# Turning chunk 2 by halves, summing one half row-block on VectorE, and another order of the first slots

## The reference

```
rowsum = adj.sum(axis=1)
d = where(rowsum > 0, rowsum ** -0.5, 0)
h = maximum(layernorm(x), 0)                      # eps 1e-5
out = relu((d[:, None] * adj * d[None, :]) @ h @ W + b)
return x + out
```

## Time and profile before

| | |
|---|---|
| median of 3 runs | 393.66 us |
| the profiled execution | 393.01 us, of it the span 391.2 us |
| TensorE (PE) busy | 383.5 us, 98% |
| VectorE (DVE) busy | 317.9 us, 81% |
| ScalarE (ACT) busy | 288.7 us, 74% |
| GpSimd (POOL) busy | 115.0 us, 29% |
| read from and written to HBM | 151.5 MB, 387 GB/s over the span |

### The profile page before, as it was taken

The page is one execution under the profiler, slowest core; times in us unless marked ns, Lnnn a source line. Parts: engine busy times, 40 slices in busy tenths (PEclk is TensorE's granted clock), DMA queues, the critical chain, the costliest instruction groups (busy, mean ns, idle before and its releaser), DMA issues. The chain is left out here.

```text
span 391.2 us, 5139 instructions
## 1 busy us (share of the span) xinstructions
PE 383.5 (98%) x1754; PEld 319.9 (82%) x1754; DVE 317.9 (81%) x312; ACT 288.7 (74%) x286; POOL 115.0 (29%) x253
## 2 busy tenths in 40 slices
PE   8998999999999999999999999999999999999995
PEld 8886888888888888888888888888888888888884
DVE  6839966899686899958689995868899497889996
ACT  2889898788787878679878867978886793346533
POOL 2470335653121226114235811422520144000000
PEclk9999999999999999999999999999999999999999
DMA  7999999999999999999999999999999965997665
GB/s 296 427 421 426 426 424 427 425 429 428 422 423 424 427 427 429 420 426 424 424 428 426 428 419 428 425 425 427 428 426 429 404 229 220 394 372 255 214 169 207
DMA packets 24216, 151.86 MB, mean 388 GB/s; under 512 B 3328, under 2 KB 3328, under 8 KB 7552
## 3 DMA queue, kind: packets, MB, share of 16 engines
q1 hardware_dynamic: 24192, 151.55, 94.5%
HBM read 147.33 MB, written 4.22 MB: 387 GB/s over the span
## 5 line engine op out<-in xcount | busy, mean ns | idle before, releaser
L441 ACT ACTIVATE hi<-at,s 128x1024 fp32r<-128x1024 f32 x112 | 122.9, 1144 | 44.5 <-issue 32.5
L928 PE MATMUL moved<-hi,G 128*128 128x512 f32 x384 | 149.6, 390 | 1.5 <-DVE acc L729 1.5
L930 PE MATMUL moved<-hi,G 128*128 128x512 f32 x384 | 149.4, 389 | 0.0
L929 PE MATMUL moved<-lo,G 128*128 128x512 f32 x384 | 149.4, 389 | 0.0
L713 DVE SCALAR_TENSOR_TENSOR lo<-at,s,hi 128x1024 fp32r<-128x1024 f32 x112 | 140.8, 1278 | 9.1 <-ACT hi L441 9.1
L732 DVE TENSOR_TENSOR acc<-moved,acc 128x1024 f32<-128x1024 f32 x84 | 102.7, 1223 | 50.5 <-PE moved L930 50.5
L431 ACT ACTIVATE nat<-nat 128x2048 f32<-128x2048 f32 x64 | 122.1, 1908 | 7.8 <-DMA nat<-in_adj 7.8
L928 PEld LDWEIGHTS moved<-hi,G 128*128 128x128 f32 x384 | 72.1, 188 | 17.0 <-DVE acc L729 1.9
L930 PEld LDWEIGHTS moved<-hi,G 128*128 128x128 f32 x384 | 72.1, 188 | 15.0
L929 PEld LDWEIGHTS moved<-lo,G 128*128 128x128 f32 x384 | 72.1, 188 | 14.9
L601 POOL TENSOR_TENSOR row_sum<-part 128x1 f32<-128x1 f32 x32 | 17.9, 561 | 183.2 <-ACT nat L431 183.0
(11 more groups left out here) (75 smaller groups left out, 253.3 us busy)
## 6 DMA issues: line engine op xcount, KB each, us to landing
nat<-in_adj SPq DMA_DIRECT2D x64, 1024.0 KB, 13.8
at<-in_adj_t SPq DMA_DIRECT2D x64, 1024.0 KB, 12.4
acc<-in_x SPq DMA_DIRECT2D x4, 512.0 KB, 7.1
nat<-d_dram SPq DMA_DIRECT2D x2, 1024.0 KB, 5.8
nat<-in_x_t SPq DMA_DIRECT2D x4, 512.0 KB, 6.0
turned<-in_x_t SPq DMA_DIRECT2D x4, 512.0 KB, 6.9
out<-nat SPq DMA_DIRECT2D x4, 512.0 KB, 5.1
turned<-in_x SPq DMA_DIRECT2D x3, 512.0 KB, 14.7
```

Source lines behind the costliest of these rows:

```text
L441: nc.scalar.activation(hi[g % RING][:, 2 * c:2 * c + 2, :], at[g % LA][:, 2 * c:2 * c + 2, :], ACT.Copy, scale=s[:, j:j + 1]).then_inc(hi_ ...
L928: nc.tensor.matmul(into[:, f, :], big, hi[g % RING][:, t, :], start=begins, stop=False)
L929: nc.tensor.matmul(into[:, f, :], big, lo[g % RING][:, t, :], start=False, stop=False)
L930: mm = nc.tensor.matmul(into[:, f, :], small, hi[g % RING][:, t, :], start=False, stop=ends)
```

## The change

Chunk 2 joins the chunks that are turned and copied in parts, by halves; TensorE turns its halves between the products of chunk 1, and ScalarE copies them around the rounding of W. Half row-block 3 is summed by VectorE (`sum_early`, with a semaphore of its own, which every waiter for sums adds to its wait). ScalarE's opening is written out anew: chunk 3's G is rounded between the two halves of slot 0, and VectorE's rest of it stands between the first and the second low part. VectorE makes three low parts ahead of the first panel's copy, where it made four, and stays one behind the former order up to slot 2; the rest of chunk 4 moves from the first half of slot 2's turn to the second. GpSimd makes the rstd of chunks 1 to 4 behind the scales of row-blocks 0 and 1.

```diff
+BY_VECTOR = (3,)
-AT_ONCE = {0: 1, 1: 2}
+AT_ONCE = {0: 1, 1: 2, 2: 2}
...
         def wait_summed(eng, m):
-            eng.wait_ge(nat_summed, m + 1)
+            dve_part = len([e for e in BY_VECTOR if e <= m])
+            at_least(eng, nat_summed, m + 1 - dve_part)
+            at_least(eng, dve_summed, dve_part)
...
             def take_part(c, t):
                 last = t + AT_ONCE[c] == BW
+                at_least(act, hW_done, c - 1)
...
-            for t in range(BW):
-                take_part(0, t)
-            take_part(1, 0)
-            take_part(1, 2)
-            round_w()
-            for c in range(AHEAD - 2):
-                if c == 2:
-                    sum_nat(2)
-                round_raw(c)
-                if c < 2:
-                    sum_nat(c)
-                if c + 2 < FIRST_PART:
-                    take_turned(c + 2)
-                else:
-                    take_high(c + 2)
-                if c == 2:
-                    sum_nat(3)
-            round_slot(0)
+            for c in range(OWN):
+                if c == 2:
+                    round_raw(0)
+                for t in range(0, BW, AT_ONCE[c]):
+                    take_part(c, t)
+                    if (c, t) == (2, 0):
+                        round_w()
+            sum_nat(0)
+            round_raw(1)
+            take_turned(3)
+            sum_nat(1)
+            round_raw(2)
+            take_high(4)
+            sum_nat(2)
+            round_tile(0, 0)
+            round_raw(AHEAD - 2)
+            round_tile(0, 1)
             round_slot(1)
-            round_raw(AHEAD - 2)
             round_raw(AHEAD - 1)
...
             scale_of(0)
-            rstd_of(1)
-            rstd_of(2)
             scale_of(1)
+            for c in range(1, AHEAD):
+                rstd_of(c)
...
-                if OWN <= j - 2 < AHEAD:
-                    rstd_of(j - 2)
...
+            def sum_early(m):
+                dve.wait_ge(nat_landed[m % LN], DMA * (m // LN + 1))
+                nc.vector.reduce_sum(part[:, m // 2, m % 2:m % 2 + 1], nat[m % LN][:, :],
+                                     axis=mybir.AxisListType.X).then_inc(dve_summed, 1)
...
-            for c in range(OWN, AHEAD):
-                take_stats(c)
-                if c == AHEAD - 1:
-                    rest_of_w()
-                rest_of_raw(c - 3)
-            rest_of_raw(AHEAD - 3)
+            take_stats(3)
+            rest_of_raw(0)
+            take_stats(4)
+            rest_of_w()
+            rest_of_raw(1)
+            sum_early(3)
+            rest_of_raw(2)
             rest_of_turned(AHEAD - 1)
-            for n in range(4):
-                subtract(n // 2, n % 2)
+            subtract(0, 0)
             rest_of_raw(AHEAD - 2)
-            piece = 4
+            subtract(0, 1)
+            subtract(1, 0)
+            piece = 3
             for g, (k, q, panels) in enumerate(SLOTS):
                 if NARROW[k] and NARROW[SLOTS[g + 2][0]]:
                     for p in range(2):
                         gather(k, 2 * q + p)
-                        if (g, p) == (2, 0):
+                        if (g, p) == (2, 1):
                             rest_of_raw(AHEAD - 1)
-                            continue
-                        for n in range(piece, 2 * g + p + 5):
+                        upto = 2 * g + p + (4 if g < 3 else 5)
+                        for n in range(piece, upto):
                             subtract(n // 2, n % 2)
-                        piece = 2 * g + p + 5
+                        piece = upto
...
             def turn_part(c, t):
-                if c == 1 and t > 0:
-                    pe.wait_ge(hT_ready, 1)
+                if c == 0:
+                    at_least(pe, part_hT_ready, part_before(c, t) - 2)
+                elif t == 0:
+                    pe.wait_ge(part_hT_ready, part_before(c, t) - 1)
                 else:
-                    at_least(pe, part_hT_ready, part_before(c, t) - (2 if c == 0 else 1))
+                    pe.wait_ge(hT_ready, c)
...
             turn_part(1, 2)
-            for c, n in ((1, 3), (2, 2), (3, 1)):
-                if n:
-                    project(c, range(n))
+            project(1, range(2))
+            turn_part(2, 0)
+            project(1, range(2, 3))
+            turn_part(2, 2)
+            project(1, range(3, 4))
+            for c, n in ((2, 2), (3, 1)):
+                project(c, range(n))
                 turn(c + 1)
                 project(c, range(n, BW))
             project_parts(4)
```

More of the change, by code:

```diff
@@ L266, in build @@
         nat_summed = sem("nat_summed")
+        dve_summed = sem("dve_summed")
         s_ready = sem("s_ready")
```

## The result

The changed kernel takes 395.55 us (median of 9 runs, 394.33 to 396.99), the kernel before 393.57 (9 runs, 393.35 to 393.97). The ratio, formed over all runs of both and not from the two medians, is 1.0044, 95% interval 1.0030 to 1.0058: slower by 1.7 us, where the medians differ by 2.0. The forecast was 1.2 us. The upper end of its range, 395.4, is 1.0044 of the 393.66 it started from: by the ratio the result lies on that end, by its median 0.15 us beyond. The profiled execution is 394.62 us with a span of 392.8, 1.61 us over the profiled one of before.

A forecast was written before the change was run, and what follows sets the result against it. TensorE, busy 98% of the span, was taken as the bound. Gaps of 1.78 us before became 3.02 after (0.11 + 0.10, 2.71, 0.10 head): 1.2 slower, 393.66 + 1.2 = 394.9 us, range 393.5 to 395.4.

The forecast's parts named there:

- Part 1, the first gap: In front of slot 1: the 1.78 us gap shrinks to 0.2 as the panel copy comes earlier, gain 1.6 us.
- Part 2, the new gap: In front of slot 3: TensorE waits for a panel copy, then chunk 4's subtraction; 2.71 us lost where nothing was.
- Part 3, the head: Opening up to slot 0: VectorE's sum of half row-block 3, 2.2 us long, makes the head 0.1 us late.
- Rival B: In the head: VectorE's sum is short, head 0.95 us earlier; 0.15 us slower, 393.8; chance 0.10.
- What hides the rest: Opening and first slots: roundings, low parts, scales, rstd and later transfers stay in time for TensorE; put at nothing.
- The sum: Whole kernel: gaps of 1.78 us before against 3.02 after, 1.2 us slower, median 394.9.
- rival D: Behind the gap at slot 3: TensorE's clock falls to half rate, adding 1.8 us, 396.7; chance 0.03.
- The granted clock stays at 1.00 over the 1.5 us gap: Earlier trace, gap in front of slot 1: no clock drop seen, cited against rival D's drop behind a 2.7 us gap.
- Rival A: In front of slot 3: the wait for chunk 4's rest doesn't bind; 1.5 us faster, 392.2; chance 0.10.
- my check that data would still be in time: First slots: low parts stay ahead of TensorE's matmuls, the fourth in time by 0.3 us.
- nothing after 35.58 us delays it: From slot 1's start to 384.50: TensorE is busy without a break, so the end moves with that stream's start.

The follow-up runs named there:

- the filled one: Changed kernel with ten 128-column matmuls of zeros in the gap ahead of slot 3: 394.48 us, ratio 1.0019 to the kernel before.
- the fastest kernel: Kernel before with the first slots' new order, chunk 5's x two slots later, half row-blocks three ahead up to slot 11: 391.59 us, 0.9952.
- the two heads: Old or new opening, both with the first slots' new order, chunk 5's x later, half row-blocks three ahead: old 391.59 us (0.9952), new 391.89 (0.9959).

## Why the prediction was right, and where it wasn't

**Part 1, the first gap: right.** 34.09 to 34.43 in place of 33.67 to 35.58, 0.11 and a restart of 0.11, where 0.11 and up to 0.10 were forecast. The four low parts and copies stood in the order and at the distances that were worked out.

**Part 2, the new gap: right to a hundredth.** 2.83 us from start to start, then 0.34, where 2.84 and 0.33 were summed from the earlier trace rows. This is the step that decides the sign, and it came from reading what `held[0]` waits for, not from any duration.

**Part 3, the head: right mechanism, small size.** Slot 0 starts at 28.83, 0.53 later, against 0.1. The sum took 2.20 from start to start, the value taken; half row-block 3 landed 15.3 us after its issue instead of 14.9, and VectorE's opening is 0.4 late already at 7.45, where it waited for x. The head used to hang on ScalarE and now hangs on a landing. How much later the new head is on average no run shows: over the profiles of all runs slot 0 starts at 28.2 to 30.8 with the old head (five of them) and at 28.4 to 29.9 with the new one (eight). The Trainium skill, "VectorE: DVE Perf Modes", section "The perf-mode tier table", gives tensor_reduce only the one-element rate. The trace agrees: 2.29 us for 2048 elements per partition, as long as the subtraction of that size in the earlier trace rows. Rival B is out. (The pitch of bn_stats that bounded it from above stands in the earlier trace rows.)

**What hides the rest: right.** Scale 1 was ready at 27.8 (forecast 27.5), the second high part at 29.0 (28.7), its low part at 30.3 (30.0), and TensorE took it at 31.6 without a wait.

**The sum: 1.2 forecast, 1.6 in the profiled execution, 1.7 by the ratio, 2.0 by the medians.** In the profiled execution the 0.4 above the forecast is the head. In the median it is rival D, to which I gave 0.03: the five lower runs have a mean 1.15 us over the kernel before's, just the forecast, the four upper ones a mean 2.6 over it. D's mechanism and price were about right (1.8 forecast, 1.6 measured) but only as a rare case; it is in about half of the executions. "The granted clock stays at 1.00 over the 1.5 us gap" said nothing of a gap of 2.7, and I let it stand for it. So the step that failed in size is the term for the clock behind the new gap, put at nothing. The range left D out, and the result lies on its upper end and not clear outside it because five of nine executions kept their clock, which is luck. The Trainium skill, "TensorE: Matmul & The Clock Gate", section "Part 1: The HAM clock gate", says that idleness of the array halves the clock. The trace agrees, in two profiles, with 0.51 and 0.54 granted behind a gap of 2.84 and 2.83 from start to start; the first profile, with a gap of 2.83 too, kept 1.00.

**Rival A would have been priced wrong.** It gave 392.2 if slot 3's wait did not bind. Without that wait the kernel takes 393.8: my check that data would still be in time looked at the low parts of the first slots against their matmuls, and not further back at VectorE's order, in which an addition that TensorE needs stands behind a low part that waits for a transfer and for ScalarE. For a later TensorE it holds that nothing further back adds to the time; for an earlier one, "nothing after 35.58 us delays it" is true with 0.4 us of room.

**What stays open.** Which executions lose clock behind the same gap. Two kernels with a gap of 1.1 to 1.3 us near 65 had one and two long runs of 12 (395.4 to 395.7), and the filled one had one of 11 (396.6), where the kernel before, with its gap of 1.5 us, had none in 76. None of these long runs is profiled, and their mean clock (0.993 to 0.996) is a weak sign: runs of 0.995 and 0.996 took only 393.6 to 393.8, one of the kernel before with 0.949 took 393.71, and in the fastest kernel's profile the clock is halved at the very end, behind the last matmul, where it costs nothing. What share of the next limit is the transfer and what share ScalarE's sums. And the head's worth by itself: the two heads differ by 0.3 us with intervals that overlap.

## What to carry to other kernels

When a consumer is moved behind another operation in an in-order queue, ask of each engine what it stands before and what that waits for: here one line moved behind a copy that could not start opened a gap of 2.7 us, longer than the one which the rest of the change closed. A gap closed early is worth only what the next limit allows; to find that limit, look for operations that stand in the queue ahead of one that the critical engine needs, not only at when its data lands. Before naming that limit, look what stands right behind it: an edit that lifts two at once does not tell which one held. And two edits that each measure as nothing can be almost 2 us together.

## What the runs showed of the hardware

An idle stretch of TensorE of 2.45 us was followed in two of the three profiles that have it by a granted clock of 0.51 and 0.54 for some 3 us, with matmuls 0.43 apart instead of 0.23, about 1.6 us lost; by their times that happened in seven of the changed kernel's 15 executions. With ten matmuls of zeros in the same stretch the ratio to the kernel before was 1.0019 instead of 1.0044 and 1.0046. Behind shorter waits (0.6 to 1.6 us in the slots, up to 2.1 in the opening) the granted clock stayed at 1.00 in every profile.
